# Mixture of experts in pairs of turns, ranks from one table and four POOL operations, and the last stores waited for later

## What is computed

```
h = h + attn(layernorm(h))
x2 = layernorm(h)                        # 12608 rows of 192
scores = sigmoid(x2 @ gate.T);  s = scores + gate_bias
group_scores = s.reshape(T, 4, 2).sum(-1)         # pairs of experts
gidx = top_k(group_scores, 2); masked = s where the group is chosen, else -inf
idx  = top_k(masked, 2);  w = scores[idx] / (sum + 1e-6)
y = sum_e cw[e] * (silu(x2 @ w1[e].T) * (x2 @ w3[e].T)) @ w2[e].T
out = h + y + (silu(x2 @ sw1.T) * (x2 @ sw3.T)) @ sw2.T
```

## Time and profile before

| | |
|---|---|
| median of 2 runs | 1679.34 us (1679.07 to 1679.62) |
| profiled execution, its own time | 1682.05 us |
| profiled execution, span from first to last instruction | 1679.4 us |
| mean granted clock of PE | 0.986 of full |
| PE busy | 1608.4 us, 96% |
| DVE busy | 1275.9 us, 76% |
| ACT busy | 986.3 us, 59% |
| POOL busy | 676.1 us, 40% |

### The profile page before, as it was taken

How to read it: one execution, slowest core, us unless ns; L and a number is a source line. 1 busy time by engine, 2 the same in 40 slices (tenths; PEclk the granted TensorE clock), 3 DMA queues, 4 the chain that set the end, 5 groups by cost and what they waited for, 6 DMA issues and landing times. The chain is left out here.

```text
span 1679.4 us, 44144 instructions
## 1 busy us (share of the span) xinstructions
PE 1608.4 (96%) x16714; PEld 1102.5 (66%) x16714; DVE 1275.9 (76%) x3610; ACT 986.3 (59%) x2038; POOL 676.1 (40%) x758
## 2 busy tenths in 40 slices
PE   5999999999999999999998699999999999999998
PEld 4777777777777777777776355555555555555555
DVE  5777777777777777777775478888888878888877
ACT  2777777777777777777766345454545454454543
POOL 2333333333333333333332145554545545455543
PEclk8999999999999999999999799999999999999999
DMA  7333333333333333333410111212121211111110
GB/s 240 71 78 78 78 78 78 78 78 78 78 78 78 78 78 78 78 78 78 106 42 19 30 42 40 56 37 59 35 62 33 56 40 43 53 40 56 34 35 16
DMA packets 97695, 108.11 MB, mean 64 GB/s; under 512 B 61323, under 2 KB 74286, under 8 KB 97358
## 3 DMA queue, kind: packets, MB, share of 16 engines
q1 hardware_dynamic: 88270, 85.83, 17.5%
q0 software_dynamic: 9216, 19.47, 7.7%
HBM read 92.44 MB, written 19.37 MB: 67 GB/s over the span
## 5 line engine op out<-in xcount | busy, mean ns | idle before, releaser
L1401 POOL TENSOR_TENSOR in_lo<-inner,in_hi 128x512 f16<-128x512 f32 (+1 forms) x225 | 259.1, 1152 | 360.8 <-ACT act L1235 348.1
L913 POOL CAST qk_strips<-qk_norm 99x768 f16<-99x768 f32 x128 | 104.9, 820 | 583.2 <-DVE qk_norm L776 583.2
L605 ACT ACTIVATE prob<-ps_sc 99x792 f32<-99x792 f32 x384 | 303.4, 828 | 5.9 <-PE ps_sc L418 2.3
L1243 ACT ACTIVATE in_hi<-inner 128x512 f16<-128x512 f32 (+1 forms) x225 | 140.2, 623 | 201.6 <-DVE inner L1335 201.6
L1353 DVE SCALAR_TENSOR_TENSOR acc<-ps_y,comb,acc 128x192 f32<-128x192 f32 (+1 forms) x700 | 242.0, 408 | 0.3 <-PE ps_y L1207 0.3
L1335 DVE SCALAR_TENSOR_TENSOR inner<-ps_h,act 128x512 f32<-128x512 f32 (+1 forms) x225 | 153.0, 680 | 116.8 <-ACT act L1235 114.2
L1235 ACT ACTIVATE act<-ps_h 128x512 f32<-128x512 f32 (+1 forms) x225 | 131.9, 586 | 184.9 <-PE ps_h L1191 184.8
L1205 PE MATMUL ps_y<-w_hi,in_hi 128*128 128x192 f16 (+1 forms) x900 | 224.6, 250 | 6.7 <-DVE acc L1353 6.4
L1207 PE MATMUL ps_y<-w_hi,in_lo 128*128 128x192 f16 (+1 forms) x900 | 221.9, 247 | 0.0
L1206 PE MATMUL ps_y<-w_lo,in_hi 128*128 128x192 f16 (+1 forms) x900 | 221.9, 247 | 0.0
L356 PE MATMUL ps_hid<-lin_hi,x_hi 128*99 128x192 f16 x768 | 194.2, 253 | 19.4 <-DVE x_lo L724 10.4
(11 more groups left out here) (167 smaller groups left out, 3809.7 us busy)
## 6 DMA issues: line engine op xcount, KB each, us to landing
xin<-xp SPq DMA_DIRECT2D x64, 594.0 KB, 4.3
x_hi<-xp POOLq DMA_DIRECT2D x64, 297.0 KB, 4.0
hidden_dram<-h SPq DMA_DIRECT2D x64, 147.0 KB
hin<-hidden_dram SPq DMA_DIRECT2D x24, 384.0 KB, 3.5
out<-acc SPq DMA_DIRECT2D x24, 384.0 KB, 2.7
w_f<-w SPq DMA_DIRECT2D x1, 2304.0 KB, 9.0
yT_hi<-y_hi SPq DMA_TRANSPOSE x100, 2.4
yT_lo<-y_lo SPq DMA_TRANSPOSE x100, 2.4
```

The source lines that it names most:

```text
L605: act.activation(prob[quad][:, places].rearrange("p h m s -> p h (m s)"), ps_sc[0:TR, places, 0:2 * SLOTS], ACT.Exp, scale=D ** -0.5 / (SQ ...
L1401: pool.tensor_tensor(in_lo[b][:, 0:N], inner[b][:, 0:N], in_hi[b][:, 0:N], ALU.subtract).then_inc(inlo_done, 1)
```

## The change

1. In the second half PE, ACT and DVE take turns two by two (`two_by_two`). PE computes the full matmuls of both turns of a pair, then the four tails, then the outer products of the pair before. `inner`, `in_hi` and `in_lo` get four buffers, `ps_y` two pairs of banks. The gate's scores share a bank with `ps_y`, at its end. 225 turns make 112 pairs and one single turn; in even groups the pairs are (0,1), (2,3), (4,5), (6,7) and (8, next 0), in odd groups (1,2), (3,4), (5,6) and (7,8). POOL still goes turn by turn, and its wait for the next silu is gone.
2. The rank comes from one DVE table of "at least" (`is_ge`). Four tensor-tensor operations (`compare`) turn it into terms, two of them reading a table with rows and columns exchanged, and a DVE row sum ends it. `compare` runs on POOL, after the `inner_rest` of turns 3 (4 x 4) and 5 (8 x 8); for group 0 it runs on DVE. The parts of `route` stand in turns 3, 5 and 7, after the older sums.
3. The routing's buffers and functions move to `MixtureRows`, so that the first half can use them: gate and tanh of group 0 come before the last image's last step, and its routing up to the second table stands in DVE's last step.
4. SP's wait for the last stores of hidden rows moves into the second half, behind the transposes of group 1.
5. `rest_of` and `normalise` of a later half move from turn 7 to 8 and from 6 to 7 in odd groups.

```diff
@@ first half: SP, PE, ACT, DVE
             sp.wait_ge(consts_b_loaded, 16 * len(consts_b))
-            for p in range(2):
-                sp.wait_ge(h2_out[p], 32 * (IMAGES // 2))
...
+                if k.c == IMAGES + 3:
+                    pe.wait_ge(v_set, IMAGES)
+                    pe.wait_ge(pieces_split, PIECES)
+                    rows.gate(pe, b_group(0), ps_gate)
             run(step)
-            pe.wait_ge(v_set, IMAGES)
-            rows.gate(pe, b_group(0), ps_gate)
...
                 if k.c == IMAGES + 3:
                     act.preload_act_table_set("silu_and_others")
+                    rows.gate_out(act, b_group(0), ps_gate)
...
+                if k.c == IMAGES + 4:
+                    dve.wait_ge(consts_b_loaded, 16 * len(consts_b))
+                    rows.route(dve, b_group(0), 0)
                 if n5.active():
                     onT_out(n5)
+                if k.c == IMAGES + 4:
+                    rows.compare(dve, b_group(0), 0)
+                    rows.route(dve, b_group(0), 1)
+                    rows.route(dve, b_group(0), 2)
@@ MixtureRows
+        ROUTE_STEPS = 15
+        ROUTE_PARTS = (0, 4, 5, 10, 11, ROUTE_STEPS)
+        compare_step = sem("compare_step")
+        tables = ((cmp4, eq4, back4, bef4, G, 4), (cmp8, eq8, back8, bef8, E, 10))
+
+        def compare(eng, g, no):
+            cmp, terms, back, before, M, steps = tables[no]
+            R = rows_of(g)
+            r = slice(0, R)
+            eng.wait_ge(route_step, g.times(ROUTE_STEPS, steps))
+            own, other = cmp[r], cmp[r].rearrange("p t i j -> p t j i")
+            earlier = before[r].unsqueeze(1).broadcast_to([R, T, M, M])
+            later = before[r].rearrange("p i j -> p j i").unsqueeze(1).broadcast_to([R, T, M, M])
+            eng.tensor_tensor(terms[r], own, earlier, ALU.mult).then_inc(compare_step, 1)
+            eng.tensor_tensor(back[r], other, later, ALU.mult).then_inc(compare_step, 1)
+            eng.wait_ge(compare_step, g.times(8, 4 * no + 2))
+            eng.tensor_tensor(back[r], later, back[r], ALU.subtract).then_inc(compare_step, 1)
+            eng.wait_ge(compare_step, g.times(8, 4 * no + 3))
+            eng.tensor_tensor(terms[r], terms[r], back[r], ALU.add).then_inc(compare_step, 1)
...
+            def at_least(cmp, values, M):
+                then(dve.tensor_tensor(cmp[r], values[r].unsqueeze(2).broadcast_to([R, T, M, M]),
+                                       values[r].unsqueeze(3).broadcast_to([R, T, M, M]), ALU.is_ge))
+            if part_no == 0:
+                at_least(cmp4, gsum, G)
+            if part_no == 1:
+                dve.wait_ge(compare_step, g.times(8, 4))
+                then(dve.tensor_reduce(rank4[r].rearrange("p t i -> p (t i)"),
+                                       eq4[r].rearrange("p t i j -> p (t i) j"), AX.X, ALU.add))
...
+            if part_no == 2:
+                at_least(cmp8, masked, E)
+            if part_no == 3:
+                dve.wait_ge(compare_step, g.times(8, 8))
+                then(dve.tensor_reduce(rank8[r].rearrange("p t i -> p (t i)"),
+                                       eq8[r].rearrange("p t i j -> p (t i) j"), AX.X, ALU.add))
@@ phase_b
+        ps_y = [[ps(f"ps_y{b}{half_no}", [128, 512]) for half_no in range(2)] for b in range(2)]
+        ps_gate = ps_y[0][1][:, 2 * C:512]
+        def two_by_two(own_work, older_work):
+            turns = [(Index(0, g, 2, GROUPS_B), e) for g in range(GROUPS_B) for e in range(NE)]
+            for i in range(0, len(turns) + 2, 2):
+                own, older = turns[i:i + 2], turns[max(i - 2, 0):i]
+                own_work(own, lambda: [older_work(g, e) for g, e in older])
@@ SP
+            for p in range(2):
+                sp.wait_ge(rows.h2_out[p], 32 * (IMAGES // 2))
@@ PE
-                    if reached(g.times(2 * NE, 2 * e + half_no - 1)):
-                        pe.wait_ge(acc_done, g.times(2 * NE, 2 * e + half_no - 1))
+                    if reached(g.times(2 * NE, 2 * e + half_no - 3)):
+                        pe.wait_ge(acc_done, g.times(2 * NE, 2 * e + half_no - 3))
+            def turn(own, older_products):
+                for g, e in own:
+                    inner_products(g, e)
+                scored = [g.back(-1) for g, e in own if e == 3 and g.back(-1).active()]
+                for following in scored:
...
+                    rows.gate(pe, following, ps_gate)
+                for g, e in own:
+                    inner_tails(g, e)
+                for following in scored:
+                    pe.wait_ge(tanh_done, following.times(1, 1))
+                older_products()
+            two_by_two(turn, outer_products)
@@ ACT
+            def turn(own, _):
...
+                for g, e in own:
+                    silu(g, e)
+                for g, e in own:
+                    inner_first(g, e)
+                for g, e in own:
+                    ahead = g.back(-2)
+                    if e == 5 and ahead.active():
+                        rows.normalise(act, ahead, 0)
+                    if e == 6 + g.c % 2 and ahead.active():
+                        rows.normalise(act, ahead, 1)
@@ DVE
+            def turn(own, older_sums):
+                for g, e in own:
+                    multiply(g, e)
+                older_sums()
+                for g, e in own:
+                    following, ahead = g.back(-1), g.back(-2)
+                    if g.c == 0 and e == 0:
+                        rows.compare(dve, g, 1)
+                        rows.route(dve, g, 3)
+                        rows.route(dve, g, 4)
+                    if e in (1, 2) and ahead.active():
+                        rows.stats_of(dve, ahead, e - 1)
+                    if e in (3, 5, 7) and following.active():
+                        for part_no in ((0,), (1, 2), (3, 4))[e // 2 - 1]:
+                            rows.route(dve, following, part_no)
@@ POOL
-                if e + 1 < NE or g.back(-1).active():
-                    pool.wait_ge(silu_done, g.times(NE, e + 2))
...
                     inner_rest(g, e)
                     if e == 3 and g.back(-2).active():
                         rows.rstds(pool, g.back(-2))
-                    if e in (6, 7) and g.back(-2).active():
-                        rows.rest_of(pool, g.back(-2), e - 6)
+                    if e in (3, 5) and g.back(-1).active():
+                        rows.compare(pool, g.back(-1), e // 4)
+                    if e == 6 and g.back(-2).active():
+                        rows.rest_of(pool, g.back(-2), 0)
+                    if e == 7 + g.c % 2 and g.back(-2).active():
+                        rows.rest_of(pool, g.back(-2), 1)
```

More of the change, by code:

```diff
@@ L245, in phase_a @@
         xlo_done = sem("xlo_done")
-        h2_out = [sem(f"h2_out{p}") for p in range(2)]
+        h2_out = rows.h2_out
         hid_done, xT_done, qk_done, v_done = sem("hid_done"), sem("xT_done"), sem("qk_done"), sem("v_done")
@@ L932, with __init__ @@
 class MixtureRows:
[L935 removed]
+    def __init__(self, nc, hidden_dram, out, sem, sb, minus_half, gate_hi, gate_lo, gbias, bef4, bef8):
         T, E, G = LANES, EXPERTS, EGROUPS
@@ L950, in __init__ @@
         h_in = [sem(f"h_in{p}") for p in range(3)]
+        h2_out = [sem(f"h2_out{p}") for p in range(2)]
         yT_in = [sem(f"yT_in{p}") for p in range(3)]
@@ L1210, in _ @@
             first = Index(0, 0, 2, GROUPS_B)
-            def body(g):
-                following = g.back(-1)
-                for e in range(NE):
+            def turn(own, older_products):
+                for g, e in own:
                     inner_products(g, e)
-                    if e > 1:
-                        outer_products(g, e - 2)
-                    elif g.back(1).active():
-                        outer_products(g.back(1), e + NE - 2)
-                    if e == 3 and following.active():
-                        rows.gate(pe, following, ps_gate)
-                if not following.active():
-                    outer_products(g, NE - 2)
-                    outer_products(g, NE - 1)
-            run(body)
+                scored = [g.back(-1) for g, e in own if e == 3 and g.back(-1).active()]
+                for following in scored:
+                    g, e = own[0]
+                    if reached(g.times(2 * NE, 2 * e - 6)):
+                        pe.wait_ge(acc_done, g.times(2 * NE, 2 * e - 6))
+                    rows.gate(pe, following, ps_gate)
[5 more added lines that the diff above has]
+            two_by_two(turn, outer_products)
         @block.scalar
@@ L1329, in multiply @@
             def multiply(g, e):
[L1330 removed]
+                N, b, q = T * rows_of(g), (g.c + e) % 2, (NE * g.c + e) % 4
                 dve.wait_ge(silu_done, g.times(NE, e + 1))
[L1333 to L1335 removed]
+                if reached(g.times(NE, e - 3)):
+                    dve.wait_ge(inlo_done, g.times(NE, e - 3))
@@ L1336, in multiply @@
```

(7 more changed lines are left out.)

199 lines of the change are left out of this document (77 added, 122 removed).

## The result

The changed kernel takes **1737.16 us** (median of 2 runs, 1736.61 to 1737.71) against 1679.34 before: ratio **1.033** (95% interval 1.031 to 1.035), 57.8 us slower. The forecast was 1706, range 1665 to 1724. It had the kernel slower by 26 us: the direction was right, the size was not. The profiled execution has a span of 1735.8 us against 1679.4 and a mean granted clock of 0.977 against 0.986.

The account below looks back on a forecast made before the run. PE's own issue sequence was taken to bound the second half. Tails -22, stall +35, clock +18 and border -5 sum to +26 on a median of 1679.34, giving 1706 us, range 1665 to 1724.

Parts of the forecast that it names:

- Tails, -22: PE, second half: changing to the half-height form once per pair saves 0.20 us in 112 pairs; -22 us, bounds -22.4 to 0.
- The stall, +35: PE waits 2.9 us in each of 12 odd groups for in_lo(6), queued behind POOL's comparison; +35 us, bounds +13 to +46.
- Four operations of 256 elements at 0.67 each, 2.8 us: POOL's 8 x 8 comparison: length of its four operations, placed between the rows for 128 and 384 elements.
- 0.9 to spare: Even groups: POOL ends in_lo(7) at 16.4 us against 17.3 needed, so the comparison costs nothing there.
- I gave it 6 us: Skill's rule for long-step reads on POOL: comparison some 0.5 us longer, sum 6 us higher; not included in the forecast.
- The gate, left at nothing: PE's gate scores in the second half: no cost for waiting on their transposes was put in the sum.
- the later normalise and rest_of cost nothing: Odd groups: both moves fit in ACT's 3 us and POOL's time after in_lo, feeding transposes a group ahead; no cost.
- The clock, +18: PE falls to half clock after the new stalls: 2.6 us in 7 of 12 groups; +18 us, bounds 0 to +40.
- The border, -5: Between the halves: earlier barrier, shorter first stretch of the second half and less half clock; -5 us, bounds -8 to +1.
- The 1 us for the moved wait: Border: moving SP's wait for the hidden-row stores lets the barrier come 1 us earlier, at most 1.6.

Follow-up runs that it names:

- e9: e6 with the last routing part (five small DVE operations) moved from turn 7 to turn 0 of the group it is for; 1657.53 us, ratio 0.986.
- e12: e9 with each turn's two tails directly behind its own full matmuls; 1673.52 us, ratio 0.996.
- e4: The changed kernel with its comparison operations reading both tables in stored order, without exchanging rows and columns; 1724.18 us, ratio 1.026.
- e1: The changed kernel with POOL's comparisons of odd groups moved behind the in_lo of the pair's second turn (turns 4 and 6); 1735.23 us, ratio 1.032.
- e5: The changed kernel with the comparison on DVE instead of POOL, in turns 3 and 5 behind the routing parts; 1704.51 us, ratio 1.014.
- e3: e1 with rest_of(0) ahead of the 8 x 8 comparison on POOL, in odd groups (turn 6) and even groups (turn 5); 1697.16 us, ratio 1.010.
- e6: e3 with normalise and rest_of of the second half at turn 6 in odd groups, ahead of the comparison; 1665.44 us, ratio 0.991.
- e8: e6 with SP's wait for the last stores of hidden rows back at the end of the first half, ahead of the barrier; 1665.59 us.
- e10: e9 with the first three routing parts between the multiplies and the sums of their pair on DVE; 1751.71 us, ratio 1.042.

## Why the prediction came out low

**Tails, -22: right.** A pair is 6.08 us; the couples follow each other closely; e9 and e12 give 16 us net and 6 in gaps.

**The stall, +35: right mechanism, mis-sized; it measured +55.** "Four operations of 256 elements at 0.67 each, 2.8 us" is the term that failed. They take 3.66: the exchanged reads are 0.64 us of it, as e4 shows, and the plain ones take 0.73 each, where the two rows that the prediction names have 0.71 halfway. The prediction counted a stall from when PE would have started, and so counted it is 3.87 us in odd groups (1.04 + 2.84) instead of 2.9, 12 us in all. The even groups, "0.9 to spare", lose 0.69, 8 us in all. Of the 1.6 us between, 0.86 is the comparison; another 0.5 is a small step of DVE in front of the table, `chosen`, which takes 0.68 us (1037.35) beside POOL's in_lo and 0.17 in the odd group (1006.28). The rule in the Trainium skill, "GPSIMD Engine Reference", section 7 (Performance pitfalls for Q7 kernels), was the better guide: it gave 0.5 us more per comparison, the trace has 0.64. Its factor of about 1.5 for a read in long steps lies between the 1.72 and 1.17 measured. I gave it 6 us and left the sum to rows that held no such read.

**The gate, left at nothing: wrong, +14.** The gate waits 11.2 us in the changed kernel, 14 by starts. Two steps of the prediction failed here. It followed the comparison to in_lo and no further: `rest_of(0)` stands behind it too, with eight transposes of about 1.3 us, 10.4 us on SP, and PE's gate at their end. That is what the gate waits for in the changed kernel, and 46.9 us in e1, where the stall is gone. And "the later normalise and rest_of cost nothing" looked at how long the operations take and not at the queue that they feed. In the changed kernel the first chain covers that mistake; e5, without a comparison on POOL, shows it at 11.5 us, and between e3 and e6, which differ by two moved operations in odd groups, it is 32 us, half clock and all.

**The clock, +18: right in sum, by two errors that cancel.** The forecast had 2.6 us in 7 of 12 double groups. The windows show 1.7 us in 11 of 12, 19 us. So the cost of one fall was too high and the count too low, and that the sum fits is luck. PE's matmuls are at half clock (1.2 GHz) from 1013.5 to 1016.8 behind the gap of 2.67 us; the windows behind the gaps of 0.53 and 0.88 us are at 1.00, and so is the one behind the gap of 2.68 us at 1137.77. In e4 a gap of 1.95 us (1454.25) was followed by half clock and one of 2.30 us (1083.23) was not. In e5, whose gaps are at most 2.1 us (40 us in sum), the clock is 1.00 from 1000 to 1600 us, and so it is in e6 and e9. No run varied the gap's length alone, and what sets the one gap apart from the 11 stays open.

**The border, -5: about right.** The first stretch gave 2.7 us and its later half-clock steps most of the rest; that all of it is 5 is what the account leaves over. The 1 us for the moved wait was nothing: the start follows POOL's last operation by 5.60 us with the wait in either place (e8).

In sum -22 + 55 + 14 + 19 - 5 = 61, against 57.8 measured; the account is good to some 3 us. Of the 32 us by which the forecast was low, some 20 are the stall, 14 the gate and 1 the clock, by the same account and with the same 3 us over. This counts costs in one trace. It doesn't say what taking one away would bring: e1 took 48 us of the waits for in_lo away and e4 15, and the gate's wait grew by 36 and by 14.

## What to carry to other kernels

When work moves to a helper engine, draw that engine's queue with what stands behind each item, and follow every item to its last consumer, through the DMA queue too: here the places of the comparison and of `rest_of` on POOL, and of `normalise` on ACT, were worth 72 us (e6), and plain reads in the comparison 13 (e4). A merged schedule saves on the bound engine and takes slack from the others; price each burst of theirs against the new slack. When one wait is removed and the time stays, read the waits again before giving up the theory: a second one of the same size may stand under it (e1, e4).

## What the runs showed of the hardware

- POOL, 256 float32 elements per partition, two inputs: 0.73 us in stored order, 0.85 with one operand's rows and columns exchanged, 1.25 with both.
- Small DVE steps on SBUF data that take 0.17 to 0.19 us alone took up to 0.84 us (e6) and 1.08 us (e10) beside POOL's in_lo, and the longest ended as POOL's operation ended (1207.22 and 1207.20 in e6), while the sums that read PSUM kept their 0.35 us each and row sums of one SBUF input their 0.2. By the Trainium skill, "GPSIMD Engine Reference", section 1 (Specifications), POOL shares its SBUF interfaces with VectorE, and VectorE operations of a two-port mode or with two SBUF inputs contend for them. This agrees for the step with two SBUF inputs (`masked`, 0.85 us in e10 and 0.19 alone); whether the stretched steps of one input run in a two-port mode no run shows.
- From POOL's last operation of the first half to PE's first matmul of the second: 5.60 us (within 0.01) in four kernels, whatever the stores did.
